# One unit, one product and one turn change places in the first attention group of each batch

## What is computed

```python
xn = _layernorm(x);  s = attention(xn)          # 16 heads of 16, causal softmax
g = _silu(ffn(xn));  x = x + s * g              # ffn: silu(gate) * up, then down
xn = _layernorm(x);  s = hyena(xn)              # projections, short filter, long convolution by FFT
g = _silu(moe(xn));  x = x + s * g              # 20 experts, 2 of them per row
```

```python
scores = jnp.einsum('bqhd,bkhd->bhqk', q, k) * SCALE + causal_bias
out = jnp.einsum('bhqk,bkhd->bqhd', jax.nn.softmax(scores, axis=-1), v)
h = jax.nn.gelu(xf @ wg1 + bg1);  logits = h @ wg2 + bg2      # the router
```

## Time and profile before

| | |
|---|---|
| three runs | 1133.52, 1143.81, 3089.38 us (median 1143.81) |
| profiled execution | 1136.37 us, its span 1134.6 us |
| TensorE (PE) | 989.7 us busy, 87% of the span |
| VectorE (DVE) | 708.9 us, 62% |
| ScalarE (ACT) | 480.1 us, 42% |
| GpSimd (POOL) | 409.6 us, 36% |
| mean granted TensorE clock | 0.924 |

### The profile page before, as it was taken

How to read it: one execution, slowest core, us unless ns; L and a number is a source line. 1 busy time by engine, 2 the same in 40 slices (tenths; PEclk the granted TensorE clock), 3 DMA queues, 4 the chain that set the end, 5 groups by cost and what they waited for, 6 DMA issues and landing times. The chain is left out here.

```text
span 1134.6 us, 19157 instructions
## 1 busy us (share of the span) xinstructions
PE 989.7 (87%) x5936; PEld 755.6 (67%) x5936; DVE 708.9 (62%) x1456; ACT 480.1 (42%) x887; POOL 409.6 (36%) x604
## 2 busy tenths in 40 slices
PE   0848999999999999999999989985699989999995
PEld 0636687577577577577577676664566668888884
DVE  5225556656667667667667655637267438999897
ACT  1413544454454454454455443543122335444441
POOL 6101331261361361361361361352100035787770
PEclk9966997999999899899899997898699999999998
DMA  4662573453463463463453551049366753234331
GB/s 148 136 108 87 77 159 131 74 117 130 62 127 130 60 129 130 59 130 130 59 112 130 80 120 57 2 168 340 108 210 207 214 193 117 98 121 130 119 92 37
DMA packets 87596, 137.23 MB, mean 121 GB/s; under 512 B 9907, under 2 KB 63347, under 8 KB 85364
## 3 DMA queue, kind: packets, MB, share of 16 engines
q1 hardware_dynamic: 69188, 101.40, 36.2%
q0 software_dynamic: 6144, 16.79, 4.8%
q10 hardware_dynamic: 12208, 18.35, 4.6%
HBM read 79.88 MB, written 55.57 MB: 119 GB/s over the span
## 5 line engine op out<-in xcount | busy, mean ns | idle before, releaser
L1459 DVE TENSOR_REDUCE Mneg<-PS 128x2 f32<-128x1024 f32 (+2 forms) x192 | 195.6, 1043 | 101.0 <-PE PS L992 101.0
L1234 ACT ACTIVATE PT<-PS 128x512 f32<-128x512 f32 (+1 forms) x384 | 170.0, 537 | 166.8 <-PE PS L1016 166.3
L1688 POOL TENSOR_TENSOR idle_p<-neghalf 128x1 f32<-128x1 f32 x128 | 25.2, 197 | 356.7 <-ACT PT L1234 356.7
L1016 PE MATMUL PS<-qs,ks 96*128 96x512 f32 (+3 forms) x512 | 141.0, 389 | 10.5 <-ACT PT L1234 5.6
L988 PE MATMUL PS<-ks,qs 96*128 96x256 f32 (+3 forms) x512 | 134.9, 376 | 2.1 <-DVE xnT L1385 1.3
L1016 PEld LDWEIGHTS PS<-qs,ks 96*128 96x128 f32 x512 | 97.1, 210 | 40.3 <-ACT PT L1234 25.6
L816 PE MATMUL PS<-xnT,Wgu 128*128 128x512 f32 x384 | 103.7, 412 | 4.3 <-ACT V L1177 2.4
L1694 POOL TENSOR_SCALAR_AFFINE_SELECT PT<-PT 128x256 f32<-128x256 f32 x256 | 100.1, 415 | 0.0
L1845 PE MATMUL PS<-Wes,xbT 128*128 x336 | 97.7, 400 | 2.4 <-issue 1.6
L988 PEld LDWEIGHTS PS<-ks,qs 96*128 96x128 f32 x512 | 88.0, 221 | 13.5 <-issue 6.9
L1029 PE MATMUL PS<-PT,V 128*32 128x512 f32 (+3 forms) x1024 | 83.2, 469 | 4.0 <-POOL PT L1694 4.0
(11 more groups left out here) (227 smaller groups left out, 1764.0 us busy)
## 6 DMA issues: line engine op xcount, KB each, us to landing
qs<-qk_parts SPq DMA_DIRECT2D x96, 128.0 KB
ks<-qk_parts SPq DMA_DIRECT2D x96, 128.0 KB
xb<-slots_in SPq DMA_DIRECT2D x84, 128.0 KB, 2.3
slots_out<-yb ACTq DMA_DIRECT2D x28, 384.0 KB, 3.2
qk_parts<-qhl SPq DMA_DIRECT2D x16, 512.0 KB, 2.7
qk_parts<-khl SPq DMA_DIRECT2D x16, 512.0 KB, 2.6
xn2T_parts<-xn2T SPq DMA_DIRECT2D x8, 1024.0 KB, 4.8
xT<-xn2T_parts ACTq DMA_DIRECT2D x7, 1024.0 KB, 5.0
```

What stands on the lines that cost most here:

```text
L1016: last = pe.matmul(PS[:, 4 + n, col:col + T - P * kt], ks[:, hd, P * kt:P * kt + P], qs[:, hd, P * kt:T], start=True, stop=True)
L1234: act.activation(PT[:, g % 2, j, 512 * n:512 * n + width], PS[:, 4 + n, 0:width], ACT.Exp, scale=SCALE).then_inc(S["exped"], 1)
L1459: dve.tensor_reduce(out=Mneg[:, 0, qt, heads[0]:heads[-1] + 1], in_=all_of, op=ALU.max, axis=AX.X, negate=True).then_inc(S["maxed"], 1)
```

## The change

In the first group of every batch but the last, TensorE's unit 5 stands ahead of the fourth product of `project_qk`. In every batch the turn of the maxima (`maxima_as_rows(b, 0)`) stands ahead of the router's first product, and the router's logits are issued after unit 4 of group 1 instead of after unit 1. On VectorE the third and fourth low parts move behind the maxima of unit 5: the third behind `parts_of_maxima`, the fourth behind the copy to `mrow`. The reading of the logits moves behind the maxima of unit 4 of group 1. SyncE's, ScalarE's and GpSimd's programs are as before.

```diff
@@ TensorE, attention
-                            if s == 1 and u == 1 and not first:
+                            if s == 1 and u == 4 and not first:
                                 route_logits(b - 1)
@@ TensorE, sequence
                     for u in range(2, NU):
-                        if not last:
+                        if not last and u < NU - 1:
                             project_qk(b + 1, (u - 2,))
                         if last and u == 4:
                             filter_step(1)
                         unit(b, 0, u)
-                    if last:
+                    if not last:
+                        project_qk(b + 1, (3,))
+                    else:
                         filter_step(2)
+                    maxima_as_rows(b, 0)
                     if not first:
                         route_hidden(b - 1, b + 1)
-                    maxima_as_rows(b, 0)
@@ VectorE, first_group
                     for u in range(2, NU):
-                        if not last:
+                        if not last and u < NU - 2:
                             split_qk(b + 1, (u - 2,))
                         maxima(b, 0, u)
                     parts_of_maxima(b, 0)
                     if last:
                         filter_rows()
+                    else:
+                        split_qk(b + 1, (2,))
                     rows_of_maxima(b, 0)
+                    if not last:
+                        split_qk(b + 1, (3,))
@@ VectorE, attention
-                            if g == 1 and u == 2 and not first:
+                            if g == 1 and u == 4 and not first:
                                 route_logits(b - 1)
```

## The result

The changed kernel took 1152.61 us (median of four runs, 1150.54 to 1153.04), the kernel before 1140.96 beside it. The ratio is 1.013, with a 95% interval of 1.009 to 1.018: slower, and within 2%. One run of the kernel before, 3089.38 us, lies far outside the rest and is not in the ratio. A second measurement of the same kernel on another chip gave 1.016 (1.009 to 1.022). The profiled execution has a span of 1151.3 us against 1134.6, TensorE is busy for 997.0 us against 989.7, and its mean granted clock is 0.917 against 0.924.

What follows compares the result with a forecast made beforehand. TensorE was taken to bound the kernel, busy 80.98 of 85.00 us per batch. The profiled 1136.4 us plus 10.6 (transfer and logits) plus 3.9 (seventh batch's clock fall) gave 1150.9, say 1151; range 1134 to 1164.

Steps and rivals of the forecast that it cites:

- Unit 5, the turn, the copy: First group, third batch: parts 1.45 us and copy 1.43 us earlier, of which 0.42 us are left when the row transfer is issued.
- The spill's data ahead of the transfer: DMA queue, first group: the row transfer `qs<-mrow` waits behind the last spill's data, so TensorE's first transposed product starts 0.5 us late.
- bound 0.4 early: Lower bound for the first transposed product: with an empty DMA queue it starts at 276.35, 0.4 us early.
- The logits: Behind unit 4 of group 1 TensorE has no idle time for them, so they cost 1.06 us per batch.
- The clock: Behind the longer idle time before the first transposed product, the seventh batch's granted clock falls too: +3.9 us.
- The sum: +1.56 us in each of six batches (+9.4), +0.5 in the first, +0.7 in the last: +10.6 us, before the clock's +3.9.
- The 0.7 for the last batch: Last batch, without spills: copy earlier, so -0.4 for the transfer and +1.06 for the logits, +0.7 us.
- The unheld transfer: Rival: the spill's data don't hold the row transfer, 0.66 us a batch; 1144.6 us, or 1140.7 without the seventh batch's fall; chance 0.17.
- The longer falls: Rival: third to sixth batch pay 6.7 instead of 3.9 us, the seventh 6.7; stretches 24 us or more; 1165 us; chance 0.15.
- Fewer falls: Rival: one long gap may leave no clock fall behind it; 1118 us without six falls, 1132 with half; chance 0.12.

## Why the prediction was right

The time (1151 said, 1152.6 measured), the direction and the mechanism of the late transfer and of the logits held. The falls of the clock were longer than the sum had them. That the total came within 2 us is partly luck: errors of both signs met in it, and the forecast stood on the profiled execution of the kernel before, 1136.4, while the median beside the changed kernel was 1141.0. From median to median the kernel lost 11.7 us, where 14.5 were forecast; from profile to profile it lost 16.7.

- **Unit 5, the turn, the copy.** Said for the third batch: turn 272.09, copy 272.65, last spill 273.60, row transfer 273.96. Measured 272.07, 272.60, 273.51, 273.97. That only 0.4 of the 1.4 us won on VectorE pass SyncE's program is what the trace shows, and moving the transfer ahead of two spills gave back the rest.
- **The spill's data ahead of the transfer.** Said 0.5 us late, bound 0.4 early; measured 0.35 late (14.91 against 14.56). My value added up two spills of 1.35 us after a start of 0.8; they ran from 273.4 to 276.0, 0.2 us better. The three places of the transfer (2.41, 2.81, 3.18 us to its user) bear the mechanism out.
- **The logits.** Said 1.06 us, taken from the earlier trace rows at 2.4 GHz, although shows the place where they go mostly at 1.2 GHz. They do hold up the next transposed product by 2.11 us there. But they cost the stretch only 1.2 to 1.5 us, by the table above, so the term was nearly right, for a reason that the prediction doesn't give. Without a fall the same place costs 273.02 - 271.70 = 1.32 us from mask product to transposed product in the version with the early transfer, against 0.14 (265.97 to 266.11) in the version that has the logits elsewhere: 1.18. The sentence that TensorE has no idle time to take them was right.
- **The clock.** The seventh batch did fall: its stretch went from 17.58 to 24.00 us, 5.1 for a fall of 13.7 us and 1.3 for the logits, where 3.9 and 1.06 were forecast. The falls of the third to sixth batch were 13.7 us long instead of 10.2, which costs 1.3 us in each (21.4 to 22.7). The sum had nothing for this; only a rival had it. The logits' new place is not needed for it: the falls were 13.7 us long in five of six batches with the logits back in their old place, on another chip. The falls of the kernel before are known from one execution, so why they were longer, and how far the change is behind it, stays open. In the second batch the fall was shorter, 13.7 us instead of 17.1, and that paid for the logits.
- **The sum.** From the second batch's first unit to the last batch's it is 532.6 us against 515.4: +17.2. The later transfer makes 2.3 of it over six batches, the six stretches 17.1 (-0.1, 2.6, 2.7, 2.8, 2.8, 6.4), and the rest of the batches -2.3, mainly the seventh, which lost two later falls of 3.4 us. The prediction had 13.3 for the same six batches. The 0.7 for the last batch didn't come: there the turn was earlier, 9.22 us after the first unit instead of 13.64, and from its first unit on the kernel was 0.6 us faster than before. 3.9 us too little in the middle and 1.7 too much at the two ends made the total fit better than its parts.
- **The rivals.** The unheld transfer is out by the 3.18 us. The longer falls happened in part: the stretches came to 24.0, which was that rival's sign, but 1.2 to 1.4 of that is the logits, and a fall of 13.7 us costs 5.1 and not 6.7. Fewer falls did not happen in the profile of this comparison (in the second one, one of the six was missing) and were most of the gain of the versions with the early transfer.

## What to carry to other kernels

A step that is made early on one engine gains nothing if another engine's program has it behind transfers that became late by the same edit: follow the moved result through the queue that ships it, both the order of issue and the data ahead of it. A piece of work moved under a low clock holds up its neighbour by its price at that clock (here 2.11 us), but if the clock comes back at the same time as without it, the stretch pays only about its price at the high clock (here 1.2 to 1.5); price the falls by their number and length, beside the work. And a wait of 1 to 2 us ahead of dense TensorE work can cost a multiple of itself by the clock (here 5 to 7 us in most batches); take it away first, here by one transfer's place in SyncE's program, for 2 to 3% in place of a loss of 1.3%.

## What the runs showed of the hardware that was not expected

- The row transfer of 16 KB took 2.41 us from issue to its user with nothing ahead, 2.81 behind one write of 512 KB issued 0.46 us before, and 3.18 behind two issued 1.34 and 0.46 us before.
- The same batch with the same idle time of 1.39 or 1.85 us ahead of the transposed products took 83.8 to 84.2 us where the granted clock stayed at 2.4 GHz and 88.8 to 91.8 where it fell to 1.2. It can do either in one execution.
- 0.9 us of additional products in that wait made the kernel faster than the changed one, 0.995 (0.991 to 1.000) against 1.013 and 1.016 of the kernel before, on different chips. The logits in the same wait, with the same 0.9 us left idle, did not keep the clock up: falls in six of six middle batches against three of six.
- A stretch with a fall of 13.7 us was 1.2 to 1.5 us longer with the logits in it, as much as one without a fall, though they took 1.89 us in the one and 1.06 in the other.
- The eight small products of the logits took 1.06 us at 2.4 GHz and 1.89 at 1.2, nearly double, though each has only 20 columns.
